# A graph kernel's filter stage: messages of the first 220 groups sorted by source block through DRAM instead of added in DRAM

## What is computed

```
h = relu(layernorm(x))
f = (softplus(edge_attr @ W1 + b1) - log 2) @ W2 + b2        # one row of 128 per edge
msg = h[dst] * f
x = x + segment_sum(msg, src)                                 # scattered by the random index
h = relu(layernorm(x))
x = x + conv(relu(conv(h)))    # conv: mean by (dst, edge_type) of h[src], times W of the type, plus root and bias
```

## Time and profile before

| | |
|---|---|
| runs, median (lowest to highest) | 7818.91 us (7816.49 to 7820.31) |
| profiled execution | 7832.82 us, its span 7831.1 us |
| busy, share of the span | PE 57%, PEld 46%, DVE 42%, ACT 38%, POOL 77% |
| costliest line | L1334 POOL, gathers: 3157.0 us, x3328 |
| second | L983 POOL, accumulating scatters: 2680.5 us, x1664 |
| chain that ended last | POOL L1334 19% of the span |

### The profile page before, as it was taken

How to read it: one execution, slowest core, us unless ns; L and a number is a source line. 1 busy time by engine, 2 the same in 40 slices (tenths; PEclk the granted TensorE clock), 3 DMA queues, 4 the chain that set the end, 5 groups by cost and what they waited for, 6 DMA issues and landing times. The chain is left out here.

```text
span 7831.1 us, 131272 instructions
## 1 busy us (share of the span) xinstructions
PE 4451.5 (57%) x25966; PEld 3596.8 (46%) x25966; DVE 3319.2 (42%) x10415; ACT 2970.8 (38%) x8043; POOL 6021.2 (77%) x5311
## 2 busy tenths in 40 slices
PE   1766667667666676666555555555544444444444
PEld 1555555555555555534444444444433333333333
DVE  6444444444444444466455555555521111111111
ACT  5444444444444444455333333333322222222222
POOL 4888888888888888855777777777767777777777
PEclk9888888888888888887566666666655555555555
DMA  8887777778887776776334433433322222222222
GB/s 271 139 133 131 133 134 131 133 132 135 132 132 133 131 131 130 129 237 209 92 102 106 105 105 104 105 105 105 102 65 56 56 55 56 56 56 56 56 56 54
DMA packets 762591, 878.30 MB, mean 112 GB/s; under 512 B 127885, under 2 KB 571125, under 8 KB 762206
## 3 DMA queue, kind: packets, MB, share of 16 engines
q0 software_dynamic: 352384, 340.33, 26.3%
q1 hardware_dynamic: 404384, 529.76, 25.1%
q10 hardware_dynamic: 5746, 7.42, 0.4%
HBM read 621.98 MB, written 255.02 MB: 112 GB/s over the span
## 5 line engine op out<-in xcount | busy, mean ns | idle before, releaser
L1334 POOL DMA_INDIRECT got<-table_dram,cidx x3328 | 3157.0, 949 | 1060.0 <-issue 1001.8
L983 POOL DMA_INDIRECT acc_dram<-total,idx x1664 | 2680.5, 1611 | 568.6 <-issue 404.0
L1382 PE MATMUL bank<-got,share 128*128 128x128 f32 x6656 | 1622.5, 421 | 1792.2 <-DMA got<-table_dram,cidx 1671.2
L1382 PEld LDWEIGHTS bank<-got,share 128*128 128x128 f32 x6656 | 1401.8, 311 | 1935.7 <-issue 1785.9
L1436 ACT ACTIVATE share<-cto_node,etcol 128x128 f32<-128x128 bf16 x3328 | 1081.5, 395 | 2777.9 <-PE bank L1382 2032.2
L816 PE MATMUL bank<-msg,same 128*128 128x129 f32 x3328 | 595.6, 335 | 903.3 <-DVE msg L948 898.2
L816 PEld LDWEIGHTS bank<-msg,same 128*128 128x128 f32 x3328 | 530.5, 238 | 1191.6 <-issue 1190.0
L948 DVE TENSOR_TENSOR msg<-bank,factor 128x512 f32<-128x512 f32 x416 | 287.8, 692 | 1574.7 <-ACT factor L883 1347.5
L877 ACT ACTIVATE total<-bank 128x258 f32<-128x258 f32 x832 | 275.3, 383 | 1552.2 <-DMA acc_dram<-total,idx 1527.5
L243 DVE SCALAR_TENSOR_TENSOR xs<-bank,mask_hi,xs 128x128 f32 x416 | 146.0, 351 | 1684.8 <-PE bank L1382 1684.8
L825 PEld LDWEIGHTS bank<-w,soft 128*128 128x128 f32 x3328 | 592.0, 250 | 30.2
(11 more groups left out here) (176 smaller groups left out, 5920.5 us busy)
## 6 DMA issues: line engine op xcount, KB each, us to landing
edges<-in_edge_attr SPq DMA_DIRECT2D x415, 256.0 KB
src_row<-in_src SPq DMA_DIRECT2D x415, 256.0 KB, 4.8
low<-rows_dram SPq DMA_DIRECT2D x416, 128.0 KB
clow<-rows_dram SPq DMA_DIRECT2D x416, 128.0 KB, 3.0
got<-table_dram,cidx POOLq DMA_INDIRECT x3328
table_dram<-made SPq DMA_DIRECT2D x98, 512.0 KB, 3.8
table_dram<-umade SPq DMA_DIRECT2D x98, 512.0 KB, 2.9
win<-split_dram SPq DMA_DIRECT2D x416, 96.0 KB
```

Of the source, the lines that this page charges most:

```text
L983: pool.indirect_dma_start(g.acc_dram[j][:, :], bass.IndirectOffsetOnAxis(ap=idx[k][:, j:j + 1], axis=0), total[k][:, j, 0:F], None, comput ...
L1334: pool.indirect_dma_start(got[k][:, j, :], None, g.table_dram[which][:, :], bass.IndirectOffsetOnAxis(ap=idx[k][:, j:j + 1], axis=0)).then ...
L1382: ins = nc.tensor.matmul(window[k], share[k][:, j, :], got[ka][:, j, :], start=j == 0, stop=j == TG - 1)
```

## The change

The filter layer is cut in two. With `UNITS = 3` and `UNIT_LAG = 10`, `NA` comes out as 220.

*Groups 0 to 219 (`plain`).* The messages are not combined and not added in DRAM. Each goes to its own row of a new array `msg_dram` (112,640 rows of 129 numbers: the message and its source index), by four indirect DMAs without accumulation for each group. The row is the message's rank in an order by source block (128 nodes a block): `prepare` makes a histogram over all 112,640 sources (one-hots by VectorE, matmuls), whose running sum, the first row of each block, is preset into the PSUM bank `ranks`; in each group 4 + 4 matmuls with a triangular matrix and its complement add the counts, and VectorE picks each edge's rank (`chosen`, `place`). `src_row`, `same`, L816, the duplicate test and `total`'s copy fall away here.

*Groups 220 to 415 (`adding`).* As before, and from step 10 on each step also treats one set of three units. A unit is 256 consecutive rows of `msg_dram`. SP loads the three (lag 10), VectorE makes one-hots of source against node (lag 11), TensorE sums by 12 matmuls (lag 12) into one bank, VectorE adds the three results to blocks of `xs` (lag 13). There are 186 sets, 558 units: 440 regular ones and 118 that catch the rows of a second block in a unit. `src_row` has two buffers instead of four. The first layer uses one bank instead of two (the other receives the unit sums).

*`prepare`* gets the histogram, `source_blocks`, `same_partition` and the unit tables; three buffers instead of four for `rest`, four instead of five for `split`. Semaphores and the `gate` are merged in places.

The diff, cut to its core:

```diff
+        fits = UNITS * (self.NG - UNIT_LAG) - self.NBX
+        self.NA = fits // (UNITS + 2) // UNROLL * UNROLL
+        self.NSET = self.NG - self.NA - UNIT_LAG
...
+def run_span(eng, start, end, tail, body, peel=PEEL):
+
+    for c in range(start, start + peel):
+        body(Step(0, c))
+    with eng.Fori(0, (end - start - peel) // UNROLL) as i:
+        for k in range(UNROLL):
+            body(Step(i, start + peel + k))
+    for c in range(end, end + tail):
+        body(Step(0, c))
...
+            def count_slabs(n0, n1):
+                for n in range(n0, min(n1, len(slabs))):
+                    c0, count = slabs[n]
+                    need(dve, s_counted, n - 1)
+                    for to, size, digit in ((one_hi[n % 2], DIG, digits[0]), (one_lo[n % 2], LOW, digits[1])):
+                        ins = v.tensor_tensor(to[:, 0:count * size].rearrange("p (c d) -> p c d", d=size),
...
+                    b = s.behind(start)
+                    if s.live(0, NG, start):
                         k = s.slot(NE, 0)
+                        load_edges(s, k)
                         if windows.own:
+                            load_low(s, k)
...
+                        k = s.slot(2, 0)
+                        need(sp, s_same, b.at(1))
...
+                    if windows.own and s.live(UNIT_LAG, NA + g.NSET, NA):
+                        k = b.slot(2, UNIT_LAG)
...
+                        need(sp, s_red, b.at(UNIT_LAG + 1))
+                        for m in range(UNITS):
+                            row = sp.value_load(so.unit_row[0:1, bass.ds(b.at(UNIT_LAG) * UNITS + m, 1)], min_val=0, max_val=NA * GE - UNIT)
+                            sp.dma_start(unit[k][:, m, :, :].rearrange("p k f -> p (k f)"),
+                                         g.msg_dram[bass.ds(row, UNIT), :].rearrange("(p k) f -> p (k f)", p=P)).then_inc(s_unit[k], 16)
...
+                        need(pe, s_sel, s.at(3) * 2 + 1)
+                        for j in range(TG):
+                            ins = nc.tensor.matmul(ranks, so.others[:, :], one_hot[s.slot(2, 3)][:, :, j], start=False, stop=True,
+                                                   skip_group_check=True)
...
+                        need(pe, s_one, s.at(2) + 1)
+                        for j in range(TG):
+                            ins = nc.tensor.matmul(ranks, so.earlier[:, :], one_hot[s.slot(2, 2)][:, :, j], start=False, stop=True,
+                                                   skip_group_check=True)
...
+                    if s.live(2, NG, start):
+                        second_layer(s)
+                        spread(s, windows)
+                    if windows.own and s.live(UNIT_LAG + 2, NA + g.NSET, NA):
+                        lag = UNIT_LAG + 2
+                        need(pe, s_unit[b.slot(2, lag)], b.use(2, lag) * (16 * UNITS) + 16 * UNITS)
+                        need(pe, s_unit_hot, b.at(lag) + 1)
+                        need(pe, s_added, b.at(lag) * UNITS)
+                        for m in range(UNITS):
+                            for k in range(UNIT // P):
+                                ins = nc.tensor.matmul(reduced[m], unit_hot[b.slot(2, lag)][:, m, k, :], unit[b.slot(2, lag)][:, m, k, 0:F],
+                                                       start=k == 0, stop=k == UNIT // P - 1)
+                        ins.then_inc(s_red, 1)
...
+                        need(dve, s_unit[b.slot(2, lag)], b.use(2, lag) * (16 * UNITS) + 16 * UNITS)
+                        need(dve, s_red, b.at(lag + 1))
+                        for m in range(UNITS):
+                            ins = v.scalar_tensor_tensor(unit_hot[b.slot(2, lag)][:, m, :, :],
...
+                    if windows.own and s.live(UNIT_LAG + 3, NA + g.NSET, NA):
+                        lag = UNIT_LAG + 3
+                        need(dve, s_red, b.at(lag) + 1)
+                        for m in range(UNITS):
+                            at = dve.value_load(so.unit_blk[0:1, bass.ds(b.at(lag) * UNITS + m, 1)], min_val=0, max_val=NBX - 1)
+                            to = g.xs[:, bass.ds(at, 1), :].rearrange("p a f -> p (a f)")
+                            need(dve, s_added, b.at(lag) * UNITS + m)
+                            v.tensor_tensor(to, to, reduced[m], ALU.add).then_inc(s_added, 1)
...
+                        apart(pool, g.gate)
+                        pool.indirect_dma_start(g.msg_dram[:, :], bass.IndirectOffsetOnAxis(ap=idx[k][:, j:j + 1], axis=0),
+                                                total[k][:, j, :], None).then_inc(s_sc[k], 16)
```

More of the change, by code:

```diff
@@ L274, in prepare @@
     bounds = [0, PART * CB, 2 * PART * CB, NBX]
-    ORDER = (0, 2, 1)
+    NTA, NMAIN, NFIX = g.NTA, g.NMAIN, g.NFIX
+    DIG = 16
+    LOW = 8
+    SLAB = P
+    slabs = [(c, min(SLAB, NTA - c)) for c in range(0, NTA, SLAB)]
+    BIG = float(1 << 20)
     with ExitStack() as ctx:
@@ L718, in filter_layer @@
         counts = bank_s[:, 0:R]
+        reduced = [bank_r[:, m * P:(m + 1) * P] for m in range(UNITS)]
+        ranks = g.bank[6][:, 0:NBX]
+        s_one = sem("f_one")
+        s_rank = sem("f_rank")
+        s_past = sem("f_past")
+        s_sel = sem("f_sel")
+        s_id = sem("f_id")
+        s_unit = [sem(f"f_unit{k}") for k in range(2)]
+        s_unit_hot = sem("f_unit_hot")
+        s_red = sem("f_red")
+        s_added = sem("f_added")
         s_edges = [sem(f"f_edges{k}") for k in range(NE)]
@@ L732, in filter_layer @@
         s_ec = sem("f_ec")
-        s_src_row = [sem(f"f_src_row{k}") for k in range(NE)]
+        s_src_row = [sem(f"f_src_row{k}") for k in range(2)]
         s_same = sem("f_same")
@@ L790, in _, with own_program, turn_edges @@
+                run_span(sp, start, NG - UNROLL, UNROLL + 4, step, peel)
+            def own_program():
+                plain()
+                adding(Windows(g, True), NA, 16)
+            if_own(sp, g, own_program, lambda: adding(Windows(g, False), 0, PEEL))
         @block.tensor
         def _(pe):
-            def program(windows):
+            def turn_edges(s):
+                need(pe, s_edges[s.slot(NE, 0)], s.use(NE, 0) * 16 + 16)
+                need(pe, s_trc, s.at(0))
+                for j in range(TG):
+                    ins = nc.tensor.transpose(bank_t[:, j * P:(j + 1) * P], edges[s.slot(NE, 0)][:, j, :], g.ident[:, :])
+                ins.then_inc(s_tr, 1)
@@ new lines, in step, with adding @@
+                    if s.live(1, NA):
+                        first_layer(s, True)
+                    if s.live(2, NA):
+                        second_layer(s)
+                        spread(s, Windows(g, True))
+                run_span(pe, 0, NA, 4, step)
+            def adding(windows, start, peel):
+                def step(s):
+                    b = s.behind(start)
+                    if s.live(0, NG, start):
+                        turn_edges(s)
+                    if s.live(1, NG, start):
+                        first_layer(s, False)
+                    if s.live(2, NG, start) and not windows.own:
@@ new lines, in adding, with step @@
+            def adding(windows, start, peel):
+                def step(s):
+                    b = s.behind(start)
+                    if s.live(0, NG, start):
+                        edges_turned(s)
+                    if s.live(1, NG, start):
+                        magnitude(s, False)
+                        exponent(s)
+                        logarithm(s)
+                    if s.live(3, NG, start):
+                        need(act, s_total, b.at(3) + 1)
+                        need(act, s_dup, b.at(3 + NTO - 1))
@@ new lines, in adding, with step @@
+            def adding(start):
+                def step(s):
+                    k = s.slot(NTO, 0)
+                    need(pool, s_idx, s.at(0) + 1)
+                    for j in range(TG):
+                        need(pool, s_sc[j], s.at(0) * 16)
+                        apart(pool, g.gate)
+                        pool.indirect_dma_start(g.acc_dram[j][:, :], bass.IndirectOffsetOnAxis(ap=idx[k][:, j:j + 1], axis=0),
+                                                total[k][:, j, 0:F], None, compute_op=ALU.add).then_inc(s_sc[j], 16)
+                run_span(pool, start, NG, 0, step)
@@ L987, in _, with own_program @@
+            def own_program():
+                plain()
+                adding(NA)
+            if_own(pool, g, own_program, lambda: adding(0))
             for j in range(TG):
```

803 lines of the change are left out of this document (541 added, 262 removed).

## The result

Before 7818.05 us (median, 7816.49 to 7820.31), after 9662.09 us (9657.05 to 9666.34): the ratio is 1.236, 95% interval 1.234 to 1.238. The profiled execution's span is 9655.3 us. The change costs 1844 us where 9440 us (1622 more) was forecast, inside the range of 8850 to 10300.

A forecast was written before the change was run, and what follows sets the result against it. It took GpSimd's accumulating scatters, 7.68 us a group, to bound the filter stage. 7832.8 + 16 - 545 + 20 - 25 + 2156 = 9455 us, put at 9440 because the profiled execution is 13.9 us above the median; range 8850 to 10300.

The forecast's parts named there:

- the three waits: Adding part: TensorE awaits VectorE's additions; SP's unit loads, `edges` behind, await TensorE's step end; first layer awaits last softplus.
- the ring: Adding part, 184 steps from step 12: SP, TensorE and VectorE work in turn, nothing overlapped; loss 2156 us.
- Plain scatter: First 220 groups: scatters without accumulation cost what a gather does, 5.2 us a group instead of 7.68; gain 545 us.
- The rival of a dear plain scatter: First 220 groups: plain scatters cost what accumulating ones do, gain shrinks by 484 us, 9920 us in all; chance 0.06.
- The first part's net: Plain groups -545 us, sorting in `prepare` +16, pipeline refill between the parts +20, GpSimd no longer trailing at the end -25.
- The ring's length: Adding part, each step: 7.15 + 6.6 + 5.6 us, say 19.4, between 16.5 and 24.4, against POOL's 7.68.
- From `spread` to the unit matmuls: Adding part, VectorE: message, compare, softplus and counts 2.55 us, then three additions and one visible register load, ending at +3.95.
- Unit matmuls: Adding part, TensorE: 12 matmuls a step at full clock, 1.6 us.
- my longest ring: Adding part: everything at half clock and loads at 4.9 us, 24.4 us a step, 10360 us in all.
- only the ring between TensorE and VectorE: Rival, adding part: loads come early enough, 10 to about 11 us a step, 7890 us in all; chance 0.06.
- POOL as the bound: Rival, adding part: POOL sets 7.68 us a step, other engines' work hidden, 7310 us in all; chance 0.08.
- My point of decision: Adding part: a step of 10.6 us, 2.9 us more than POOL's, decides between faster and slower.

The follow-up runs named there:

- the experiment without adding: Kernel before, with its filter-stage scatters no longer accumulating (unsorted rows, sums left out): 7073.74 us, 0.906 times before.
- without units: Changed kernel with unit loads, one-hots, matmuls and additions left out, sums incomplete: 7284.53 us, 0.932 times before; on the slower chip 8980.77 us, 1.000.
- the version with early additions: Changed kernel with VectorE's three additions moved ahead of the message: 10240.4 us, 1.140 times before, on the slower chip.
- the reordered one: Changed kernel with unit loads one step later, additions first with block numbers read ahead, one-hots at VectorE's step end: 7409.83 us, 0.947 times before.
- the version with both moves: Changed kernel with unit loads one step later and additions ahead of the message: 7802.87 us, 0.998 times before; on the slower chip 9472.8 us, 1.055.
- the version with four units: The reordered one with `UNITS = 4`, so 252 plain and 164 adding groups: 7539.16 us, 0.964 times before.

## Why the prediction was right

- **The counts of the three waits** gave the structure, and the trace shows it link by link: unit loads 0.84 us after the unit matmuls, `edges` behind them, unit matmuls released by the third addition. Taking either wait out of the ring shortens the step by 6.0 to 6.6 us; with no wait closed within one step it falls to 8.2. In the changed profile POOL is busy 75% in the first part (about 80% was forecast) and 30% in the second (below 40%).
- **Plain scatter:** 5.2 us a group forecast, 5.21 measured; taking the gather as the nearest row was right, and the experiment without adding shows why: direction and row order matter little, adding does. My 0.2 us for stretching has about the right size (the pitch of 1.303 us against 1.26 in an undisturbed stretch is 0.17 us a group), but that VectorE is what stretches a scatter no run shows. The rival of a dear plain scatter is out. The first part's net, -545 + 16 + 20 - 25 = -534 us, stands beside 532 us measured without units; its pieces were off and cancel, which is luck. The filter stage's first load was issued at 199.00 us instead of 165.13, so `prepare` took +34, not +16 (inside my 0 to +40). Between the parts POOL idled 7.7 us, not 20, and the adding part without units runs at 7.55 us a group, not 7.68.
- **The ring's length:** 19.35 us forecast, 20.47 measured; 184 x 1.1 = 206 us is nearly the whole difference of 222. By its terms: wait for `edges` after the unit matmuls 7.15 forecast, 6.92 measured. Burst of TensorE 6.6 forecast; in the step shown 6.20. From `spread` to the unit matmuls 3.95 forecast; TensorE's idle time there is 4.56 as a mean: I let two of the three register loads hide and one show, but two show, 0.48 and 0.55 us between the additions. Unit matmuls 1.6 forecast, 2.85 as a mean (the 12 above take 2.67): this is the term that was most mis-sized. I had applied the half clock to the burst after the 7 us wait and not to the unit matmuls after a wait of 4.4 us, though the earlier trace rows show it after 5 us; their granted clock was 0.56 in the step shown. In the version with early additions, without that wait, they take 1.58 us. One slip in the range: my longest ring, 24.4 us, gives 10360 us, which its upper end of 10300 leaves out.
- **The Trainium skill**, "DMA: Bandwidth & Descriptors", Rules for kernel authors (issue early, wait late): the runs agree. With the three unit loads moved one step and nothing else, `edges` is issued early again, which was worth 9680 - 8479 = 1200 us. The same page's Anatomy of one DMA gives its figure for DMAs that GpSimd issues, and the loads here are SP's; by it the landing was an estimated 2.6 us. In the step shown it was 2.8, and my 3.3 was too long. The load of the earlier trace rows was the first one, but it was not alone as I had it: SP had issued five more before it landed.
- **The rivals:** only the ring between TensorE and VectorE (10 to 11 us a step) isn't what the changed kernel does; POOL as the bound is what the reordered one comes near, not the changed one. My point of decision, a step of 10.6 us, fits: at 10.34 us the version with both moves is 0.2% under the kernel before.

## What to carry to other kernels

Before adding stages to a pipelined step, write down for each new wait which step's event it needs and what stands behind it in the same queue; two engines that wait for each other's events of the same step turn the step into a sum of everything. Here the order of three blocks and their register loads was worth 2270 us (9680 to 7410), and the unit work itself 125 (7410 against 7285). TensorE began at half clock after both idle stretches of this ring (granted 0.51 in the first matmuls after 6.6 us of idle, 0.56 in the unit matmuls after 4.4), so price what follows such a stretch from rows at the half level, after every stretch of the ring, and don't expect a shortened wait to come back whole.

## What the runs showed of the hardware

- **The same kernel on another chip took 15% longer** (8975.09 us against 7818 to 7824, each within 0.4%). The steps of the ring were not what differed: they were within 1% on both (13.89 and 13.99, 10.26 and 10.34 us), and so was the adding part without units (7.55 us). In the version without units it was the plain part and the convolutions; of the kernel before there is no trace from that chip. The version without units there, to be set beside its window from 200 us above:

```profile
200.00:1000.00 800.00, 554.70 (x4231) 439.56 (x4232) 440.11 (x1188) 329.36 (x655) 410.64 (x426) 0.83 0.38 104
...
DVE total L1307 <- remote: 285.3, 90, 6.7
ACT edges_t L1203 <- remote: 266.1, 68, 9.1
...
7000.00:7800.00 800.00, 224.81 (x1056) 204.04 (x1056) 126.02 (x396) 182.12 (x660) 500.83 (x525) 0.57 0.16 46
```

  426 scatters instead of 613, each still 964 ns (410.64/426), with VectorE and ScalarE waiting 3 to 4 us at a time for something that the trace calls remote. The last row is the second convolution: 525 gathers in 800 us, each 954 ns (500.83/525), where the kernel before had 800 in 1000. What this is wasn't tried and stays open. There the plain part gains nothing to pay for the rest: without units the ratio is 1.000, on the other chip 0.932.
- **An indirect scatter of 128 rows costs 0.975 us (516-byte rows) or 1.013 us (512) plain and 1.55 to 1.66 us adding.** The difference is time in which POOL is busy.
- **A register load in front of an instruction costs SP and VectorE about 0.7 us.** SP's three unit issues shrink from 2.67 to 1.37 us without the two between them, 0.65 each; VectorE idles 2.19 us for three in a row (264.8/121) and 2.82 for four (290.4/103). Between two additions 0.48 to 0.57 us of it show. They stand in no busy time, and made VectorE the bound of the version with four units.
- **Scatters stretched from 1583 to 1662 ns** when unit work ran beside them in the reordered version, and not in the version with both moves (1560 ns) nor in the one with four units (1556 ns), whose steps are longer. Why is open.
